# Choosing experts during cross-attention and scattering token records with indirect stores, in a decoder layer on one Trainium2 core

## The chip, the cores and the metric

The kernel runs on one core of a Trainium2 chip. The metric is the time of one execution on the device in microseconds (us), lower is better. A core has TensorE (PE; its weight loads are listed as PEld), VectorE (DVE), ScalarE (ACT) and GpSimd (POOL), each with its own instruction stream, and a queue SP (SyncE) that only issues DMAs. POOL also issues DMAs, among them the indirect ones, whose rows are picked by a list of indices in SBUF. Work on different engines is ordered by semaphores alone.

## What is computed

A decoder layer over 16 sequences ("rows") of 256 tokens with 256 features: local and global self-attention, then cross-attention to 120 context positions per row, then a mixture of experts. Only the last part and the way into it matter here. With x the tokens after cross-attention:

```python
xf = layernorm(x).reshape(-1, 256)             # 4096 tokens
logits = xf @ router_w.T                       # 8 experts
probs = softmax(logits)
top_p, top_i = top_k(probs, 2)
top_p = top_p / sum(top_p)                     # the two shares of a token
cw = sum(top_p[..., None] * one_hot(top_i, 8), axis=1)
for e in range(8):
    h = silu(xf @ w1[e].T) * (xf @ w3[e].T)
    out = out + cw[:, e:e + 1] * (h @ w2[e].T)
x = x + out
```

## The kernel before

Four stages follow one another, each a block at whose end all engines meet: `self_attention`, `cross_attention`, `route`, `expert_tiles`, and a last copy of the sums to the output.

`cross_attention` runs a software pipeline over rows b = 0 to 17; every engine has its own hand-written order of calls in that loop (`sync_program`, `gpsimd_program`, `tensor_program`, `scalar_program`, `vector_program`). In iteration b the scores of row b are made in four units s = 0 to 3: PE `scores` (L1201), DVE `maxima` (mask L1486, row maximum L1489), PE `subtract_max` (L1208), ACT `exponentials` (L1383), PE `turn` and `values` (L1221, L1233). Row b-1 is finished beside it: `divide`, `turn_att`, `project`, `residual` (DVE L1506). Row b-2 is normalised for the experts on POOL (`row_deviations` L1116, `apply_row_norm` L1127), turned (`turn_row` L1263), and multiplied by the router weights (`logits` L1276, in spare columns of a score bank). DVE's `copy_logits` (L1466) is put in front of `maxima(b, 0)` and takes row b-3. The query of row b+2 is split in three bf16 parts on POOL (L1140 to L1144), stored by SP (L1045), and loaded back in a stacked form (`stack_q`, L1038); `scores(b + 1, 0)` on PE comes right after `logits(b - 2)` and waits for the stacked loads of its row. SP also loads masks, expert weights and values, stores the rows for the experts, and in its iteration 4 issues eight small DMAs of `load_routing` (L1024 to L1032).

`route` (L1569) starts when all 4096 x 8 logits are in SBUF. DVE forms probabilities, takes the top two (L1661, L1664), makes one-hot rows `hot`, and with two PE products counts how many tokens of each expert come before each token; a prefix sum and the starts of the experts' regions give every token a slot in a list of 71 tiles of 128 slots (each expert's part is padded to whole tiles). Then token number and share are moved to their slots by one-hot products: for four groups of 16 token columns DVE builds `tile_hot` (L1712), `lane_hot` (L1714) and `entry` (L1717), POOL the second half of `entry` (L1621), and PE adds up 64 products (L1635). The results are `slot_row` (which token is in a slot, L1728), `slot_share`, and `tile_expert`. Nearly every DVE operation is wrapped in `step`, which makes the next one wait for its end.

`expert_tiles` handles the 71 tiles in order: POOL gathers 128 token rows (L1769), PE computes (L1807 to L1835), DVE scales by the share, and POOL adds the result to the sums with an indirect accumulating store (L1783). It can't start until `slot_row` is complete.

## Time and profile before

| | us |
|---|---|
| median of 3 runs | 1341.86 (1338.96 to 1342.02) |
| the profiled execution, its own time | 1334.86 |
| its span in the profile | 1332.9 |
| PE busy | 1164.3 (87%) |
| DVE busy | 604.5 (45%) |
| POOL busy | 593.7 (45%) |
| ACT busy | 523.9 (39%) |

The span is the time from the first to the last instruction of the profile; the stages stand in it one after the other, so a share of busy time over the whole span says little of any one of them. The profile's page cuts the span in 40 slices of 33.3 us each:

```profile
PE   3699999999999984899999994369999999999991
DVE  1355655556554541777777774832112211211220
POOL 6433444333443105466666422334555555555541
```

Each digit is the busy share of one slice in tenths. Cross-attention fills about slices 16 to 24, `route` most of slice 25 and part of 26, the experts the rest.

### The profile page before, as it was taken

To read this page: it belongs to the slowest core of one execution; us is meant where nothing else is said; L and a number is where in the kernel's file an instruction comes from. 1 tells how busy PE (TensorE), PEld (TensorE's weight loads), DVE (VectorE), ACT (ScalarE), POOL (GpSimd) and SP (SyncE) were. 2 spreads that over 40 slices of the span, in tenths; PEclk is the share of its full clock that TensorE was granted. 3 is DMA by queue.
4 is the path that set the end of the run, shared out by engine and by line. 5 is a ranking of instruction groups with operands and counts; after the bars stand their busy time and mean duration, and the time that the engine had idled before them with its cause. 6 is when DMAs were issued, how large, how long until landed. Compare 5 with 4: busy or idle time off the path is not lost. (4 is left out here: it accounts for less than half of the span.)

```text
span 1332.9 us, 27531 instructions
## 1 busy us (share of the span) xinstructions
PE 1164.3 (87%) x10384; PEld 873.8 (66%) x10384; DVE 604.5 (45%) x1081; ACT 523.9 (39%) x841; POOL 593.7 (45%) x800
## 2 busy tenths in 40 slices
PE   3699999999999984899999994369999999999991
PEld 2578787887888773677777773346666666666660
DVE  1355655556554541777777774832112211211220
ACT  1355555455554541666666651012222222222220
POOL 6433444333443105466666422334555555555541
PEclk9699999999999997899999997689999999999996
DMA  6472442625425105566666641002222222222224
GB/s 175 142 185 81 120 139 58 178 78 137 116 65 154 37 2 147 164 180 185 178 183 176 196 130 56 0 20 40 45 44 48 48 44 45 48 48 43 45 40 138
DMA packets 171325, 131.87 MB, mean 99 GB/s; under 512 B 58784, under 2 KB 160672, under 8 KB 171136
## 3 DMA queue, kind: packets, MB, share of 16 engines
q1 hardware_dynamic: 155216, 108.76, 29.4%
q0 software_dynamic: 13632, 18.62, 8.6%
q10 hardware_dynamic: 2352, 2.75, 0.7%
q8 instruction: 87, 1.43, 0.5%
q14 instruction: 38, 0.31, 0.1%
HBM read 90.31 MB, written 43.97 MB: 101 GB/s over the span
## 5 line engine op out<-in xcount | busy, mean ns | idle before, releaser
L704 ACT ACTIVATE sa_probs<-ps_scores 128x1024 f32<-128x1024 f32 x128 | 131.1, 1024 | 158.9 <-PE ps_scores L451 158.8
L1783 POOL DMA_INDIRECT sum_rows<-y,to_row x71 | 113.6, 1600 | 179.1 <-DVE y L1891 166.4
L1884 DVE TENSOR_TENSOR gate<-ps_scores,silu 128x512 f32<-128x512 f32 x71 | 49.1, 692 | 263.4 <-ACT silu L1862 263.4
L1862 ACT ACTIVATE silu<-ps_scores 128x512 f32<-128x512 f32 x71 | 42.4, 598 | 315.8 <-PE ps_scores L1817 315.8
L1817 PE MATMUL ps_scores<-w1s,xgT 128*128 x284 | 135.4, 600 | 2.3 <-ACT xgT L1856 2.3
L1835 PE MATMUL ps_out<-xres,ggT 128*128 x568 | 134.6, 380 | 1.6 <-DVE y L1891 1.6
L1817 PE MATMUL ps_scores<-w3s,xgT 128*128 x284 | 133.5, 592 | 0.0
L1835 PEld LDWEIGHTS ps_out<-xres,ggT 128*128 128x128 f32 x568 | 102.4, 190 | 13.2 <-issue 2.2
L837 DVE TENSOR_REDUCE sa_rowmax<-ps_scores 128x8 bf16<-128x1024 f32 x64 | 78.3, 1224 | 67.2 <-PE ps_scores L437 67.2
L837 DVE TENSOR_REDUCE sa_rowmax<-ps_turn 128x8 bf16<-128x1024 f32 x64 | 78.4, 1225 | 57.5 <-PE ps_turn L442 56.8
L1817 PEld LDWEIGHTS ps_scores<-w3s,xgT 128*128 128x128 f32 x284 | 54.1, 191 | 68.4 <-issue 68.4
L1486 DVE COPY_PREDICATED_SCALAR ps_scores<-zero,masked_score 128x960 f32 x64 | 77.2, 1207 | 17.2 <-PE ps_scores L1201 17.1
L451 PE MATMUL ps_scores<-neg_ident,sa_rowmax 128*128 128x128 bf16 x1024 | 79.6, 221 | 4.8 <-DVE sa_rowmax L837 4.8
L1383 ACT ACTIVATE xa_probs<-ps_scores 128x960 f32<-128x960 f32 x64 | 62.3, 973 | 54.6 <-PE ps_scores L1208 54.0
L1769 POOL DMA_INDIRECT xg<-xn_rows,from_row x71 | 71.9, 1013 | 22.1 <-POOL from_row L1765 20.0
L1817 PEld LDWEIGHTS ps_scores<-w1s,xgT 128*128 128x128 f32 x284 | 54.2, 192 | 41.2 <-issue 37.6
L285 POOL TENSOR_SCALAR rstd<-mv 128x2 f32<-128x2 f32 x16 | 3.6, 224 | 170.3 <-DVE mv L813 170.3
L1489 DVE TENSOR_REDUCE xa_rowmax<-ps_scores 128x8 bf16<-128x960 f32 x64 | 74.1, 1158 | 2.2
L1891 DVE TENSOR_SCALAR y<-ps_out,tile_share 128x256 f32<-128x256 f32 x71 | 34.3, 484 | 80.3 <-PE ps_out L1835 71.1
L1221 PEld LDWEIGHTS ps_turn<-ident,xa_probs 128*120 128x120 f32 x512 | 60.2, 138 | 11.1 <-issue 0.4
L451 PEld LDWEIGHTS ps_scores<-neg_ident,sa_rowmax 128*128 128x128 bf16 x1024 | 63.8, 99 | 5.3 <-DVE sa_rowmax L837 5.3
L1221 PE MATMUL ps_turn<-ident,xa_probs 128*120 128x128 f32 x512 | 67.1, 274 | 0.0
(210 smaller groups left out, 2368.9 us busy)
## 6 DMA issues: line engine op xcount, KB each, us to landing
xqs<-q_scr SPq DMA_DIRECT2D x96, 128.0 KB, 2.6
qs<-w_scr SPq DMA_DIRECT2D x42, 256.0 KB, 4.1
ks<-w_scr SPq DMA_DIRECT2D x42, 256.0 KB, 4.0
q_scr<-qp SPq DMA_DIRECT2D x16, 384.0 KB, 3.8
xks<-k_scr SPq DMA_DIRECT2D x48, 120.0 KB, 3.3
w_scr<-wp SPq DMA_DIRECT2D x7, 768.0 KB, 3.7
gs<-g_scr SPq DMA_DIRECT2D x48, 96.0 KB, 2.5
w1s<-in_w1T SPq DMA_DIRECT2D x16, 256.0 KB, 3.7
```

What stands on the lines that cost most here:

```text
L451: mm = pe.matmul(m.scores[s % 2][:, h, :], rowmax[s % 2][:, h:h + 1].broadcast_to((P, P)), m.neg_ident[:], start=False, stop=(h % 4 == 3), ...
L704: act.activation(probs[s % 2][:], m.scores[s % 2][:], ACT.Exp, scale=SCALE).then_inc(exped, 1)
L837: dve.tensor_reduce(rowmax[s % 2][:], m.turn[:] if kind else m.scores[s % 2][:], AX_X, ALU.max)\
L1221: mm = pe.transpose(m.turn[0:KX, h, :], probs[s % 2][:, h, 0:KX], m.ident[:])
L1383: act.activation(probs[s % 2][:, :, 0:KX], m.scores[s % 2][:, :, 0:KX], ACT.Exp, scale=SCALE)\
L1486: dve.copy_predicated(sc, zero[b % 2][:, n, :].unsqueeze(1).broadcast_to((P, HU, KX)), masked_score[:].unsqueeze(2).broadcast_to((P, HU, K ...
L1489: dve.tensor_reduce(rowmax[s % 2][:], sc, AX_X, ALU.max).then_inc(maxed, 1)
L1769: pool.indirect_dma_start(xg[i][:], None, m.xn_rows, bass.IndirectOffsetOnAxis(ap=from_row[i][:], axis=0))\
L1783: pool.indirect_dma_start(m.sum_rows, bass.IndirectOffsetOnAxis(ap=to_row[i][:], axis=0), y[i][:], None, compute_op=ALU.add).then_inc(y_ad ...
L1817: mm = pe.matmul(h_ps[r % 2][:, j:j + 1, :], xgT[r % 2][:, k, :], w[:, bass.ds(expert * DT + k, 1), :], start=(k == 0), stop=(k == DT - 1))
L1835: mm = pe.matmul(y_ps.unsqueeze(1), gT[r % 2][:, k, :], m.w2s[:, bass.ds(expert * HT + k, 1), :], start=(k == 0), stop=(k == HT - 1))
L1884: dve.tensor_tensor(gate[r % 2][:], h_ps[r % 2][:, 1, :], silu[r % 2][:], ALU.mult).then_inc(gate_done, 1)
```

## The change

Routing is spread over cross-attention. Tokens are taken in nine batches: (0,1), (2,3), ... (12,13) of two rows each, and rows 14 and 15 alone. For each batch k:

- DVE `choose(k)`: the top two logits of each token tile, their numbers, the difference of the two logits (the share is formed from it later), one-hot rows, their sum `sel`. It stands after `maxima(b, 3)` in the even iterations b = 4 to 14.
- PE `count(k)`: in bf16, one product with a triangular matrix and some with ones (8 for two rows, 4 for one), after `logits(b - 2)` and before `scores(b + 1, 0)` in the same iterations; it waits for `choose(k)`.
- DVE `copy_counts(k)` in front of `maxima` of the next row, and `place(k)` after `maxima(b, 2)` in the odd iterations: slots within fixed regions, 32 tiles for each expert.
- POOL `dispatch(k, i)`: for each row four indirect stores (two token tiles, two choices) of 128 records of 8 bytes (token number, logit difference) into a DRAM table, at the end of its iterations 5 to 16; 64 in all.

The last three batches are handled at the loop's end. The table is first filled with blank records (three stores of SP in iteration 2), `load_routing` moves from SP's iteration 4 to 0, and POOL gets `set_tables` in iteration 1. `route` keeps only: tiles of each expert from the running counts, the list of table tiles in use, one indirect gather of 71 table tiles, two PE transposes, and the shares from the logit differences.

```diff
         def load_routing():
...
+        def store_blank():
+            tab = m.table.rearrange("(r l) c -> r (l c)", l=P)
+            sp.wait_ge(blank_made, 1)
+            for r in range(0, N_TAB, P):
+                n = min(P, N_TAB - r)
+                sp.dma_start(tab[r:r + n, :], blank[0:n].rearrange("p l c -> p (l c)")).then_inc(spares_stored, 16)
@@ sync_program
-            if b == 4:
+            if b == 0:
                 load_routing()
+            if b == 2:
+                store_blank()
@@ gpsimd_program
+        def dispatch(k, i):
+            r0, rows = batches[k]
+            pool.wait_ge(slotted, k + 1)
...
+            for t in range(NT * (r0 + i), NT * (r0 + i + 1)):
+                for j in range(TOP):
+                    pool.indirect_dma_start(m.table, bass.IndirectOffsetOnAxis(ap=slot_i[:, t, j:j + 1], axis=0),
+                                            m.rec[:, t, j, :], None).then_inc(m.dispatched, 16)
@@
+            if b == 1:
+                set_tables()
+            if 5 <= b <= NB:
+                dispatch((b - 5) // 2, (b - 5) % 2)
+            if b == NB:
+                dispatch(LAST - 2, 0)
+                dispatch(LAST - 2, 1)
+        dispatch(LAST - 1, 0)
+        dispatch(LAST, 0)
@@ tensor_program
+        def count(k):
...
+            pe.wait_ge(chosen, k + 1)
+            pe.wait_ge(exped, min(UPR * (r0 + 4) + 3, UPR * NB))
+            pe.matmul(space(1, T), before[:], sel[:, 0:T, :], start=True, stop=False, skip_group_check=True)
+            for t in range(T - 1):
+                pe.matmul(space(2 + t, T - 1 - t), ones[:], sel[:, t:t + 1, :].broadcast_to((P, T - 1 - t, E)),
+                          start=False, stop=(t == T - 2), skip_group_check=True)
+            for t in range(T):
+                mm = pe.matmul(space(0, 1), ones[:], sel[:, t:t + 1, :], start=(t == 0), stop=(t == T - 1),
+                               skip_group_check=True)
+            mm.then_inc(counted, 1)
@@
+            if b == NB + 1:
+                count(LAST - 1)
...
                 values(b - 1, 3)
+            if b == NB:
+                count(LAST - 2)
             if done:
                 turn_row(b - 2)
...
                 logits(b - 2)
+            if 4 <= b < NB and b % 2 == 0:
+                count(b // 2 - 2)
             if more:
                 scores(b + 1, 0)
...
+        count(LAST)
@@ vector_program
+        def choose(k):
...
+            for t in range(T):
+                ins = dve.max(top[:, t, :], logit[:, t0 + t, :])
+            step(ins)
+            for t in range(T):
+                ins = dve.max_index(top_id[:, t, :], top[:, t, :], logit[:, t0 + t, :])
+            step(ins)
+
+            dve.tensor_tensor(m.rec[:, t0:t0 + T, 0, 1:2], top[:, 0:T, 0:1], top[:, 0:T, 1:2], ALU.subtract)
+            dve.tensor_tensor(m.rec[:, t0:t0 + T, 1, 1:2], top[:, 0:T, 1:2], top[:, 0:T, 0:1], ALU.subtract)
+            step(dve.tensor_copy(idf[:, 0:T, :], top_id[:, 0:T, 0:TOP]))
+            step(dve.tensor_tensor(hot[:, 0:T].rearrange("p t j e -> p (t j) e"),
...
+            dve.tensor_tensor(sel[:, 0:T, :], hot[:, 0:T, 0, :], hot[:, 0:T, 1, :], ALU.add).then_inc(chosen, 1)
+
+        def place(k):
...
+            step(dve.tensor_tensor(posn[:, 0:T, :], counts[:, 1:1 + T, :],
+                                   m.base[:].unsqueeze(1).broadcast_to((P, T, E)), ALU.add))
+            step(dve.tensor_tensor(m.base[:], m.base[:], counts[:, 0, :], ALU.add))
...
+            dve.tensor_copy(slot_i[:, t0:t0 + T, :], slotf[:, t0:t0 + T, :]).then_inc(slotted, 1)
@@
+            if b == NB:
+                choose(LAST - 2)
             if old:
                 divide(b - 1, 0)
...
                 maxima(b, 2)
+            if 5 <= b < NB and b % 2 == 1:
+                place((b - 5) // 2)
             if old:
                 residual(b - 1, 0)
             if some:
                 maxima(b, 3)
+            if 4 <= b < NB and b % 2 == 0:
+                choose(b // 2 - 2)
+            if b == NB:
+                copy_counts(LAST - 2)
+                place(LAST - 2)
             if old:
                 divide(b - 1, 1)
...
+        choose(LAST - 1)
+        copy_counts(LAST - 1)
+        place(LAST - 1)
+        copy_logits(NB - 1)
+        choose(LAST)
+        copy_counts(LAST)
+        place(LAST)
@@ route, gpsimd_program
+        pool.wait_ge(source_done, 1)
+        pool.wait_ge(m.dispatched, 16 * TOP * TILES)
+        pool.indirect_dma_start(records[:].rearrange("r l c -> r (l c)"), None, m.table.rearrange("(r l) c -> r (l c)", l=P),
+                                bass.IndirectOffsetOnAxis(ap=source_i[0:N_ST, :], axis=0)).then_inc(records_in, 16)
@@ route, tensor_program
+        pe.wait_ge(records_in, 16)
+        pe.transpose(ids_ps, records[:, :, 0], m.ident[0:N_ST, 0:N_ST])
+        pe.transpose(z_ps, records[:, :, 1], m.ident[0:N_ST, 0:N_ST]).then_inc(turned, 1)
```

## Rows read from the trace of the kernel before

**Rows 1.** Windows of the three stages: stretch, length, engines' busy us (count), clock, DMA.

```profile
525.00:823.00 298.00, 271.21 (x2856) 213.91 (x2856) 208.91 (x356) 180.82 (x251) 155.88 (x178) 0.97 0.58 167
823.00:880.00 57.00, 22.00 (x132) 20.28 (x132) 49.09 (x162) 0.42 (x1) 16.34 (x5) 0.66 0.00 1
880.00:1310.00 430.00, 416.49 (x1562) 259.65 (x1562) 83.46 (x142) 97.34 (x214) 221.29 (x355) 0.99 0.27 44
```

**Rows 2.** Timeline at the ends of route: start, us, engine, line, operation [idle <-releaser].

```profile
822.75 0.17 DVE L1466 COPY logits<-ps_scores 128x16 f32<-128x16 f32 x1 [7.39 <-PE ps_scores L1276]
...
841.23 0.17 DVE L1684 TENSOR_SCALAR count_i<-scan 128x8 int32<-128x8 f32 x1
841.43 0.17 DVE L1685 TENSOR_SCALAR tiles_i<-count_i 128x8 int32<-128x8 int32 x1
...
879.44 0.20 DVE L1728 TENSOR_SCALAR slot_row<-empty 128x71 int32<-128x71 f32 x1
880.15 0.19 POOL L1765 COPY from_row<-slot_row 128x1 int32<-128x1 int32 x1 [7.07 <-SPq L1899]
```

**Rows 3.** Groups of VectorE's instructions in route: line, shapes, count, busy us, mean ns.

```profile
L1664 DVE FIND_INDEX8 top_id<-top,prob 128x8 uint32<-128x8 f32 x32 | 4.4, 160 | 0.0
...
L1661 DVE MAX8 top<-prob 128x8 f32<-128x8 f32 x32 | 2.3, 152 | 0.0
```

**Rows 4.** Timeline of one steady row, PE and DVE around `scores(b + 1, 0)`.

```profile
695.09 0.42 DVE L1506 TENSOR_TENSOR xres<-ps_misc,xres 128x256 f32<-128x256 f32 x1 [2.54 <-PE ps_misc L1253]
...
696.67 1.16 DVE L1489 TENSOR_REDUCE xa_rowmax<-ps_scores 128x8 bf16<-128x960 f32 x1
...
697.33 0.96 PE L1276 MATMUL ps_scores<-routerT_sb,xbT 128*128 128x8 f32 x8
...
698.14 0.58 PE L1201 MATMUL ps_scores<-xks,xqs 96*128 96x120 bf16 x8
...
698.81 0.17 DVE L1466 COPY logits<-ps_scores 128x16 f32<-128x16 f32 x1 [0.36 <-PE ps_scores L1201]
...
701.90 0.43 DVE L1506 TENSOR_TENSOR xres<-ps_misc,xres 128x256 f32<-128x256 f32 x1 [0.59 <-PE ps_misc L1253]
```

**Rows 5.** Timeline, `copy_logits` of rows 5, 8 and 9: idle time before it.

```profile
664.78 0.17 DVE L1466 COPY logits<-ps_scores 128x16 f32<-128x16 f32 x1 [1.83 <-PE ps_scores L1201]
...
716.68 0.17 DVE L1466 COPY logits<-ps_scores 128x16 f32<-128x16 f32 x1 [1.22 <-PE ps_scores L1201]
...
734.09 0.17 DVE L1466 COPY logits<-ps_scores 128x16 f32<-128x16 f32 x1 [0.75 <-PE ps_scores L1201]
```

**Rows 6.** Timeline of one row, POOL's wait before a row, the split, SP's store.

```profile
703.48 0.23 POOL L1116 TENSOR_SCALAR brstd<-bmv 128x2 f32<-128x2 f32 x1 [5.23 <-DVE bmv L1476]
...
731.17 1.17 POOL L1144 TENSOR_TENSOR qp<-xrest,qp 128x512 bf16<-128x512 f32 x1
...
735.10 0.42 SPq L1045 DMA_DIRECT2D q_scr<-qp  x1
```

**Rows 7.** The two indirect DMAs by line: ns min/median/max; and landing.

```profile
L1769 POOL DMA_INDIRECT xg<-xn_rows,from_row x71: 974/1012/1242, 880.9 to 1284.6; - x71
...
DMA to landing us min/median/max: 2.7/2.8/3.5
...
L1783 POOL DMA_INDIRECT sum_rows<-y,to_row x71: 1562/1601/1644, 904.4 to 1308.9; - x71
...
DMA to landing us min/median/max: 3.5/3.8/4.0
```

**Rows 8.** Timeline of the last rows of cross-attention, VectorE and POOL.

```profile
804.48 0.25 DVE L1495 RECIPROCAL xrec<-ps_misc 128x16 f32<-128x16 f32 x1
...
805.73 2.44 POOL L1127 TENSOR_SCALAR xb<-xres,bmv,brstd 128x256 f32<-128x256 f32 x2
...
815.39 0.23 POOL L1116 TENSOR_SCALAR brstd<-bmv 128x2 f32<-128x2 f32 x1 [7.21 <-DVE bmv L1476]
...
816.52 2.44 POOL L1127 TENSOR_SCALAR xb<-xres,bmv,brstd 128x256 f32<-128x256 f32 x2
```

More of the change, by code:

```diff
@@ L962, in cross_attention @@
     zeros = sb("zeros", [P, D])
+    before_f = sb("before_f", [P, P])
+    before, ones = sb("before", [P, P], BF16), sb("ones", [P, P], BF16)
+    iota_p = sb("iota_p_sb", [P, P])
+    token1 = sb("token1_sb", [P, TILES])
+    blank = sb("blank", [P, P, 2])
+    logit = sb("logit", [P, TILES, E])
+    top = sb("top", [P, R * NT, E])
+    top_id = sb("top_id", [P, R * NT, E], U32)
+    idf = sb("idf", [P, R * NT, TOP])
+    hot, place_of = (sb(n, [P, R * NT, TOP, E]) for n in ("hot", "place_of"))
+    sel = sb("sel", [P, R * NT, E], BF16)
+    counts = sb("counts", [P, 1 + R * NT, E])
+    posn = sb("posn", [P, R * NT, E])
+    slotf = sb("slotf", [P, TILES, TOP])
+    slot_i = sb("slot_i", [P, TILES, TOP], I32)
     xb = [sb(f"xb{i}", [P, NT, D]) for i in range(2)]
@@ L1485, in maxima @@
                 copy_logits(b - 3)
+            if s == 0 and b > 4 and b % 2 == 1:
+                copy_counts((b - 5) // 2)
             dve.copy_predicated(sc, zero[b % 2][:, n, :].unsqueeze(1).broadcast_to((P, HU, KX)),
@@ L1581, in route @@
[L1581 to L1585 removed]
+    room = sb("room", [P, E])
     count_i = sb("count_i", [P, E], I32)
     tiles_i = sb("tiles_i", [P, E], I32)
[L1588 removed]
+    tiles_e = sb("tiles_e", [P, E])
@@ L1589, in route @@
     cum = [sb("cum0", [P, E]), sb("cum1", [P, E])]
+    behind = sb("behind", [P, E])
+    skipped = sb("skipped", [P, E])
+    lane = sb("lane", [P, 1])
+    source = sb("source", [P, 1])
+    source_i = sb("source_i", [P, 1], I32)
     passed = sb("passed", [1, N_ST, E])
     expert_f = sb("expert_f", [1, N_ST, 1])
-    lane_hot = [sb(f"lane_hot{i}", [P, GROUP, P]) for i in range(2)]
-    tile_hot = [sb(f"tile_hot{i}", [P, GROUP, N_ST]) for i in range(2)]
-    entry = [sb(f"entry{i}", [P, GROUP, 2, N_ST]) for i in range(2)]
@@ L1624, in tensor_program @@
[L1624 to L1637 removed]
+    records = sb("records", [N_ST, P, 2])
```

229 lines of the change are left out of this document (95 added, 134 removed).

## The prediction

> **What bounds the kernel now.** I first cut the span into stages with the view of windows [rows 1]. In cross-attention PE is busy for 271 of 298 us at nearly the full clock: it is the bound there. In the routing stage (823 to 880) VectorE is busy for 49 of 57 us and PE for 22, with DMA at 0.00: a stage bound by a chain of VectorE steps. In the experts' stage PE is busy for 416 of 430 us. So a change in `route` is worth what it takes from that stage's 57 us, and anything put into cross-attention costs in full where it makes PE wait.
>
> Next, the timeline at the ends of `route`. The last `copy_logits` starts at 822.75 and ends at 822.92; the last DVE step that makes `slot_row` is at 879.44, and the first instruction of the experts' stage, POOL's copy of the indices, starts at 880.15 [rows 2]. Between 822.92 and 880.15 lie 57.2 us. The end of that stretch is what the change moves; the experts' work behind it is not touched (same 71 tiles), so it moves as one block.
>
> **What `route` still costs.** Its DVE part up to the list of table tiles is a chain of 17 small steps (`room`, `lane`, `count_i`, `tiles_i`, `tiles_e`, a copy, six of the prefix sum, and five for `source_i`). Two such steps of the old chain start 0.20 us apart [rows 2]: 17 x 0.205 = 3.5 us, with some 0.3 us for the block's begin. Then the gather of 71 table tiles: an indirect gather costs POOL 1.0 us and lands 2.8 us after issue, 3.5 us at most [rows 7]; with the way to PE I take 3.2. Two small transposes: 0.7. Then nine short operations with one on ACT among them, `slot_row` to the last share: 2.3 us by the same step and a little more for 71 columns. From that to the experts' first copy 0.5, as now (879.64 to 880.15) [rows 2]. Together 10.5 us in place of 57.2, a gain of 46.7, if nothing were added elsewhere.
>
> **What is added behind row 15.** Here the chain gets longer, and the price of an indirect store to 8-byte records decides; the trace has none such. The nearest rows are the gather at 1.01 us and the accumulating store of 1 KB rows at 1.60 us [rows 7]. It can't be had for nothing, since POOL builds 128 descriptors in either; so 1.0 to 1.6, and I take 1.2: it has no accumulation and one small piece a record, which is nearer to the gather. Walked through with the times of before [rows 8]:
> - `choose(6)` now stands ahead of `divide(15, 0)` at 804.48, but row 14's norm is started at once and ends at 805.73 + 2.44 = 808.17. POOL then has `dispatch(5, 1)`, 4 stores, 4.8 us, to 813.0. `dispatch(6)` needs `place(6)`, which stands behind choose, count and `residual(15, 0)`, at about 812.4: ready in time. Its 8 stores take 9.6 us, to 822.6.
> - Only then come `row_deviations(15)` and `apply_row_norm(15)`, which before ran from 815.39 to 818.96, 3.57 us [rows 8]: now they end at 826.2, 7.2 us later. Before, the way from there to the last logits in SBUF was 822.92 - 818.96 = 4.0 us: 830.1.
> - `choose(8)` for two tiles 1.4 us, `count(8)` 0.7, `copy_counts` and `place(8)` 1.4: 833.6. `dispatch(8)`, 4 x 1.2 us: 838.5. `dispatch(7)` fits before it (826.2 to 831.0).
>
> So `route` starts at 838.5 in place of 822.9, and the experts at 838.5 + 10.5 = 849.0 in place of 880.15: 31.1 us earlier. The last store lands, by the longer row of 3.8 us, about 841.1; the wait for it is hidden behind the 17 steps, which end at 842.3. Sixteen stores are on this path (4 + 8 + 4), so 1.0 or 1.6 us a store gives -34.3 or -24.7.
>
> **What is added to the row loop.** One row takes 17.0 us. DVE has three waits for PE in it, 2.54, 0.59 and 0.36 us, 3.5 in all [rows 4].
> - `place(k)` (five steps, 1.1 us) falls into the wait of 2.54, `copy_counts` into that of 0.59: nothing, and if the first cover were gone, 1.1 us each for six batches.
> - `choose(k)` with `count(k)` is another matter. DVE ends the row maximum of unit 3 at 696.67 + 1.16 = 697.8. `choose` then has 4 maxima and 4 index searches: 2.3 us for 32 is 0.07 each after a first of 0.15, and 4.4 for 32 is 0.14 each [rows 3]: 0.38 + 0.65, then two subtractions, a copy, the one-hot rows and `sel`, 0.2 each with the step's gap: 1.9 us, to 699.6, and 0.1 to PE. But PE has the logits of row b-2 from 697.33 on and starts `scores(b + 1, 0)` at 698.1 [rows 4]. Queued behind the wait on PE are these scores and all after them, for which ACT and DVE wait in turn. So PE stands 1.6 us and spends about 0.7 on eight bf16 products of at most 32 columns (the row at 698.14 is eight larger ones, 0.58 us). 2.4 us in each of six batches: +14.4. Bounds: 1.9 if `choose` is shorter, 4 if the delayed `divide` and maxima pass the delay on.
> - Something comes back. `scores(b + 1, 0)` now sometimes waits for the stacked queries: `copy_logits` has 1.83, 1.22 and 0.75 us of idle before it where the usual value is 0.36, 2.7 us too much in all [rows 5, 4]. `load_routing` leaves SP's iteration 4, ahead of these places, and PE's rows get longer while SP's work does not, so these waits go: -2.7 (bounds 0 and -2.7). In iterations 0 and 2 SP gets eleven issues more, of 0.42 us or so each [rows 6], some 5 us; SP waits for POOL's split there and no `copy_logits` has come yet. I cost them at nothing; without that cover a late query would cost up to 5 us once.
> - `dispatch` in the loop: 4 stores a row, 4.8 us, against POOL's wait of 5.23 us before the next row's norm [rows 6]: nothing. If a store costs more, there are 2.8 us further before SP waits for the split (732.34 to 735.10 [rows 6]): it bites from (5.2 + 2.8) / 4 = 2.0 us a store.
> - `set_tables` (five short operations) and two memsets lie in POOL's waits too: nothing.
>
> **Sum**, on the profiled execution of 1334.86 us: -31.1 + 14.4 - 2.7 = -19.4, that is 1315.5. The median of the runs shown is 7.0 us above it; on it the change gives 1341.9 - 19.4 = 1322.5.
>
> **Rivals.**
> 1. *The stores starve.* POOL's descriptors for an indirect store advance only while VectorE is idle. In the trace indirect DMAs run only in the experts' stage, where VectorE is busy for 83 of 430 us [rows 1]; in cross-attention it is busy for 209 of 298. Idle there are 3.5 us a row [rows 4], less 1.6 for half a batch of choosing and placing: 1.9, while four stores need at least 4.1. Each of twelve rows would stretch by 2.2 us, at 2.6 us a store: +26, 1349. It turns the change into a loss from 2.4 us a store on in the loop, (2.4 - 2.0) x 4 x 12 = 19. Against it: VectorE's long operations in the row loop, mask and row maximum, work on PSUM, and so did the one beside which the stores of the experts' stage held their 1.6 us. The Trainium skill has this as a rule (SBUF — State Buffer, section "SBUF: two separate sides": while VectorE runs an operation in a mode with two ports, GpSimd is locked out and can't write descriptors; the section after it has such a DMA go from about 0.62 to 3.1 us). By that figure, an estimate of that page, four stores would take 12.4 us a row and the kernel would be slower; no row of this case shows the lock, since no indirect DMA here runs beside such an operation.
> 2. *The delay spreads.* DVE has 3.5 us of slack in a row, of which `choose` takes 1.9 at one place, ahead of `divide(b - 1, 1)`; if PE then waits again for `att` or the maxima, a batch costs 4 us in place of 2.4: +9.6, 1332. For it: the two engines hand work to and fro in every unit. Against it: PE's own delay of 2.4 us covers the 1.9 of DVE.
> 3. *The count is nearly free.* If PE makes up the standing time by working off what it was late with (its 271 of 298 us leave 27 [rows 1]), six batches cost 0 to 1 us each: 1310. Against it: most of those 27 us are in the last rows, where nothing is left to make up with.
> 4. *It doesn't do what it says*: the experts start hardly earlier, because the gather from the table or a late store takes the place of the one-hot products; it would need over 20 us there: 1342.
>
> **How the numbers follow.** Forecast 0.60, rival 1 0.11, rival 2 0.13, rival 3 0.10, rival 4 0.06. The forecast's own bounds: 1.0 us a store and 1.9 us a batch, 1322.5 - 3.2 - 3.0 = 1316; 1.6 a store and nothing back from SP, 1322.5 + 6.4 + 2.7 = 1332. The range reaches into rivals 2 and 3 and, with the scatter of the runs shown (3 us), becomes 1308 to 1337; left out are rivals 1 and 4 and the edge of the others, 0.19. A measurement of this kernel can tell about 0.3%, 4 us, from no change. Faster: forecast, rivals 2 and 3, a little of 4: 0.83. Same: 0.07. Slower: 0.10.
>
> **What would show it.** In the profile of the changed kernel: the experts' first gather 12 to 25 us earlier; between the last logits and it some 20 us; PE idle of 1 to 2 us ahead of `count` six times, with "chosen" by DVE as the releaser; POOL's indirect stores at 1.0 to 1.6 us each, back to back behind row 14's norm; no wait of POOL over budget, that is the norm of the next row starting without delay. I am wrong if a store takes over 2 us, if a pair of rows grows by 4 us or more, or if `dispatched` is waited for at length in `route`.

## The result, and the profile after it

The changed kernel takes 1360.2 us (median, 1354.1 to 1365.9), the kernel before 1340.6 beside it: ratio 1.0146, 95% interval 1.0095 to 1.0197. It is slower by some 20 us where 19 less were forecast. The profiled execution took 1362.9 us, its span is 1361.0.

The view of windows by stage, as [rows 1]: stretch, length, busy us of PE, its weight loads, DVE, ACT, POOL, then clock, DMA share, GB/s.

```profile
531.00:879.20 348.20, 293.94 (x2916) 229.42 (x2916) 232.72 (x534) 182.19 (x251) 215.88 (x242) 0.89 0.54 144
879.20:910.00 30.80, 0.77 (x6) 0.51 (x6) 9.51 (x45) 0.26 (x1) 6.88 (x6) 0.50 0.03 5
910.00:1340.00 430.00, 416.33 (x1562) 259.63 (x1562) 83.43 (x142) 97.40 (x214) 220.98 (x355) 0.99 0.27 44
```

The routing stage fell from 57 to 31 us. Cross-attention grew from 298 to 348: PE has 23 us more of busy time at a mean clock of 0.89 instead of 0.97, and 27 us more of standing. The experts' stage has the same length.

The timeline of the changed kernel around a choice and its count (start, us, engine, line, operation, idle time before it and its releaser), which answers to [rows 4]:

```profile
616.20 1.16 DVE L1636 TENSOR_REDUCE xa_rowmax<-ps_scores 128x8 bf16<-128x960 f32 x1
...
616.85 0.96 PE L1342 MATMUL ps_scores<-routerT_sb,xbT 128*128 128x8 f32 x8
617.27 0.36 DVE L1583 MAX8 top<-logit 128x8 f32<-128x8 f32 x4
...
618.96 0.19 DVE L1598 TENSOR_TENSOR sel<-hot 128x32 bf16<-128x32 f32 x1
...
619.25 0.18 PE L1357 MATMUL ps_scores<-sel,before 128*128 128x32 bf16 x1 [1.45 <-issue]
...
619.61 0.58 PE L1265 MATMUL ps_scores<-xks,xqs 96*128 96x120 bf16 x8
...
620.66 1.66 PE L1285 MATMUL ps_turn<-ident,xa_probs 128*120 128x128 f32 x8
...
624.94 0.42 DVE L1653 TENSOR_TENSOR xres<-ps_misc,xres 128x256 f32<-128x256 f32 x1 [2.06 <-PE ps_misc L1317]
```

The choice takes DVE from 617.27 to 619.15, the 1.9 us that were costed. PE stands 1.45 us and counts in 0.4. Behind that its granted clock falls: it is 1.00 up to 620.60 and 0.59 from there to 622.40, in part the lower of its two levels (1.2 instead of 2.4 GHz). Eight transposes take 1.66 us there, which take 1.03 in a row without a count.

From one `residual` to the next a row has two segments, 10.2 and 6.8 us long in the kernel before (the short one in [rows 4], 695.09 to 701.90). Some of them in the changed kernel, by windows (columns as above):

```profile
674.45:687.30 12.85, 8.75 (x82) 6.75 (x81) 5.85 (x8) 5.84 (x8) 7.73 (x8) 0.87 0.66 183
687.30:697.50 10.20, 10.02 (x103) 7.74 (x101) 7.45 (x15) 6.81 (x10) 7.49 (x9) 1.00 0.39 111
697.50:707.88 10.38, 8.91 (x90) 7.12 (x89) 7.56 (x27) 4.34 (x6) 7.02 (x8) 0.84 0.81 164
...
718.07:731.09 13.02, 9.58 (x82) 7.38 (x81) 5.86 (x9) 5.41 (x8) 7.73 (x8) 0.74 0.76 210
...
761.82:770.90 9.08, 7.19 (x86) 5.84 (x84) 5.76 (x8) 4.30 (x6) 7.01 (x8) 1.00 0.85 258
770.90:782.49 11.59, 10.86 (x95) 8.69 (x96) 7.56 (x15) 7.44 (x11) 7.50 (x9) 0.85 0.41 113
```

Three patterns stand here. 697.50 is the short segment of a row with a count, 10.4 us instead of 6.8. At 674.45 and 718.07 there is no count, and the segment has 12.9 and 13.0 us. From 761.82 on a pair has 9.1 and 11.6 in place of 6.8 and 10.2. Set beside the segments of the kernel before, the loop from the first `residual` of the second row to the last one is 45.0 us longer: 20.7 in the six segments with a count; 10.8 in the two long ones; 7.9 in two pairs of the third kind; 5.7 in the rest.

What lies behind the long segments is on SP. Its timeline ahead of the first of them (the issues of the DMA queue) and PE's first late scores, and then SP's waits (total us, times, longest), the last line that of the kernel before:

```profile
637.80 0.40 SPq L1076 DMA_DIRECT2D q_scr<-qp  x1
649.74 4.68 SPq L1069 DMA_DIRECT2D xqs<-q_scr  x5
...
658.61 11.68 SPq L1069 DMA_DIRECT2D xks<-k_scr  x6
...
671.61 0.38 SPq L1076 DMA_DIRECT2D q_scr<-qp  x1
675.09 4.65 SPq L1069 DMA_DIRECT2D xqs<-q_scr  x6
...
681.93 0.61 PE L1265 MATMUL ps_scores<-xks,xqs 96*128 96x120 bf16 x8 [2.52 <-DMA xqs<-q_scr]
```

```profile
SPq L1069 <- DMA q_scr<-qp: 76.9, 15, 11.5
SPq L1069 <- DMA xks<-k_scr: 22.9, 10, 4.1
...
SPq L1038 <- DMA q_scr<-qp: 61.2, 16, 7.4
```

SP sends the split queries to the scratch tensor and waits for the confirmation before it reads them back stacked. At 637.80 it waits 11.5 us (in the kernel before 7.4 at most). All that it does is then late: the keys until 670.3, the next row's queries only at 671.61, and PE waits for them at 681.93. The same happens from 683.52 (stacked from 692.50 on) to the scores at 724.90. The copies of logits behind these scores stood idle for 3.27 and 4.18 us, where [rows 5] show 0.75 to 1.83.

The windows of that wait (columns as above, the last two DMA share and GB/s), the last line being of the kernel before, behind its store at 652.74:

```profile
641.00:644.00 3.00, 2.06 (x18) 1.58 (x18) 1.53 (x4) 0.92 (x2) 1.94 (x3) 1.00 0.70 207
...
645.00:649.70 4.70, 4.54 (x47) 3.45 (x46) 4.60 (x9) 3.80 (x6) 4.01 (x6) 1.00 0.00 0
...
656.10:656.70 0.60, 0.60 (x5) 0.49 (x3) 0.60 (x1) 0.27 (x1) 0.60 (x1) 1.00 0.10 28
```

For the last 4.7 us of the wait the profile shows no packet under way; only the confirmation is missing. In the kernel before SP goes on at 656.68, when the transfers have only just ended.

The tail, from POOL's timeline and then all engines, which answers to [rows 8] and [rows 2]:

```profile
856.44 1.09 POOL L1180 DMA_INDIRECT table<-rec,slot_i  x1 [0.18 <-issue]
...
870.49 0.96 POOL L1180 DMA_INDIRECT table<-rec,slot_i  x1 [0.30 <-issue]
...
879.03 0.17 DVE L1559 COPY logit<-ps_scores 128x16 f32<-128x16 f32 x1 [9.99 <-PE ps_scores L1342]
...
882.13 0.17 DVE L1611 CAST slot_i<-slotf 128x4 int32<-128x4 f32 x1
...
886.37 0.96 POOL L1180 DMA_INDIRECT table<-rec,slot_i  x1 [0.30 <-issue]
895.25 0.17 DVE L1781 TENSOR_SCALAR room<-iota_e_sb 128x8 f32<-128x8 f32 x1 [12.96 <-PEq L1703]
...
898.52 0.16 DVE L1797 TENSOR_TENSOR source_i<-source,lane 128x1 int32<-128x1 f32 x1
...
898.99 2.08 POOL L1760 DMA_INDIRECT records<-table,source_i  x1 [11.66 <-DVE source_i L1797]
...
906.44 0.40 PE L1765 MATMUL ps_misc<-ident,records 71*128 71x71 f32 x1 [25.42 <-DMA records<-table,source_i]
...
910.05 0.19 POOL L1848 COPY from_row<-slot_row 128x1 int32<-128x1 int32 x1 [8.98 <-SPq L1982]
```

Twelve stores stand back to back ahead of row 15's norm, 1.27 us apart. The last store ends at 887.33, and the routing stage's first step starts at 895.25. The gather is issued at 898.99 and PE has its records at 906.44.

### The profile page after: what moved, and what is told of

Its sections match the earlier page's. It is cut to its first block and busy times, and to the rows that moved or that the text cites. A ratio compares the mean times of both kernels' runs of the same rounds, so it can differ in the third digit from the quotient of the medians.

```text
span 1361.0 us, 27550 instructions
## 1 busy us (share of the span) xinstructions
PE 1171.1 (86%) x10318; PEld 872.8 (64%) x10318; DVE 588.7 (43%) x1141; ACT 525.3 (39%) x841; POOL 644.1 (47%) x867
## 5 line engine op out<-in xcount | busy, mean ns | idle before, releaser
L1633 DVE COPY_PREDICATED_SCALAR ps_scores<-zero,masked_score 128x960 f32 x64 | 77.3, 1207 | 18.5 <-PE ps_scores L1265 18.4
L1285 PEld LDWEIGHTS ps_turn<-ident,xa_probs 128*120 128x120 f32 x512 | 67.1, 150 | 17.6 <-issue 9.1
L1285 PE MATMUL ps_turn<-ident,xa_probs 128*120 128x128 f32 x512 | 75.0, 295 | 3.1 <-ACT xbT L1502 3.1
L1180 POOL DMA_INDIRECT table<-rec,slot_i x64 | 63.6, 994 | 22.6 <-issue 16.9
L1484 ACT COPY xa_probsT<-ps_turn 120x1024 f32<-120x1024 f32 x64 | 64.8, 1012 | 13.6 <-PE ps_turn L1285 12.8
```

The lines of the kernel that those rows point to most:

```text
L1180: pool.indirect_dma_start(m.table, bass.IndirectOffsetOnAxis(ap=slot_i[:, t, j:j + 1], axis=0), m.rec[:, t, j, :], None).then_inc(m.dispat ...
L1285: mm = pe.transpose(m.turn[0:KX, h, :], probs[s % 2][:, h, 0:KX], m.ident[:])
L1484: act.copy(probsT[s % 2][0:KX, :, :], m.turn[0:KX, :, :]).then_inc(turn_read, 1)
L1633: dve.copy_predicated(sc, zero[b % 2][:, n, :].unsqueeze(1).broadcast_to((P, HU, KX)), masked_score[:].unsqueeze(2).broadcast_to((P, HU, K ...
```

## The experiments

Each kernel was timed beside the kernel before; ratios are to that one, with the 95% interval. Kernels with less work or other data in the table say so in their expectation.

### Which part of the change costs: stores or choice

**The stores of the loop left out** (`e1_no_loop_stores`):

```
-            if 5 <= b <= NB:
-                dispatch((b - 5) // 2, (b - 5) % 2)
```

> The changed kernel without the 48 indirect stores of batches 0 to 5 (the records of rows 0 to 11 are missing from the table, so most tokens get no expert); choose, count and place stay as they are, and the last 16 stores too. Theory A (the 8-byte stores are confirmed late, and SP's store of the query parts, issued beside them, is confirmed late with them, so the next row's scores wait): in the trace of the changed kernel the odd iterations take up to 6 us more than before; they return to 17.0 us, SP waits about 4 us for each store of the query parts in place of 9 to 12, and the time falls by about 20 us, from 1360 to 1340. Rival B (SP is late because choosing and counting shift the row loop, with or without stores): within 5 us of 1360. The even iterations keep their 3.6 us more under both.

Measured: 1332.7 us, 0.996 (0.993 to 0.999). The segments are 10.2 to 10.4 with a count and 6.8 without (8.0 once); SP's waits for `q_scr` are 56.6 us, longest 6.2. So the 48 stores cost some 27 us although POOL has the time for them. By the traces 24 of these are in the loop: 12.2 in the two segments in which SP's confirmation is late, 8.3 in the pairs of the third kind, the rest in small pieces.

**The choice, count and placing of the loop left out** (`e2_no_loop_choose`), the stores kept and sent to places fixed beforehand:

```
-            if 4 <= b < NB and b % 2 == 0:
-                choose(b // 2 - 2)
```

> The changed kernel with all 64 stores, but without choose, count, copy_counts and place for rows 0 to 11, whose records go to fixed slots spread over the eight regions (so the routing of these rows is not computed). Theory A: the even iterations lose their 3.6 us more (six times, 21.6 us), the odd ones keep waits for stacked queries; SP still waits 9 to 12 us for the store of the query parts; time about 1340. With PE's rows shorter these waits could even grow. Rival B: with choosing and counting gone, SP is in time again, and the time is about 1318.

Measured: 1377.2 us, 1.0305 (1.027 to 1.034), slower than with the choice, and pairs of segments of 20 to 24 us instead of 17. That went against any theory in which a store has one price. What the stores cost depends on where their records go.

**The choice one place earlier** (`e3_choose_early`): behind `maxima(b, 2)` and `place`, ahead of `residual(b - 1, 0)`:

```
+            if 4 <= b < NB and b % 2 == 0:
+                choose(b // 2 - 2)
             if old:
                 residual(b - 1, 0)
             if some:
                 maxima(b, 3)
-            if 4 <= b < NB and b % 2 == 0:
-                choose(b // 2 - 2)
```

> The changed kernel, complete, with choose(k) moved ahead of residual(b - 1, 0), into VectorE's wait of 2.5 us, so that count(k) finds it done. If the order wait is the cause of the even iterations' 3.6 us (1.6 of standing, 0.7 of products, the rest PE at the half clock after it): they fall to 0.5 to 1 us, -16 us, 1344. If SP's late stacked queries are a bound of their own, part of it returns as longer waits there: 1350. If the order wait is not the cause: 1360.

Measured: 1350.5 us, 1.0095 (1.007 to 1.012). The segments with a count fall to 7.0 to 8.1 us (one to 10.1), but others rise to 13.8, and SP's waits for `q_scr` to 93.9 us. DVE can hide the choice; a part of what that frees goes into SP's lateness.

### Where the records lie

**Records 64 bytes apart** (`e5_pitch64`) instead of 8; the gather at the end still takes whole rows of the table, now 71 of 8 KB:

```
+PITCH = 16
-        m.table = nc.dram_tensor("table", [N_TAB * P, 2], F32, kind="Internal").ap()
+        m.table = nc.dram_tensor("table", [N_TAB * P, PITCH], F32, kind="Internal").ap()
-            dve.tensor_copy(slot_i[:, t0:t0 + T, :], slotf[:, t0:t0 + T, :]).then_inc(slotted, 1)
+            dve.tensor_scalar(slot_i[:, t0:t0 + T, :], slotf[:, t0:t0 + T, :], float(PITCH // 2), None, ALU.mult)\
+                .then_inc(slotted, 1)
```

> The changed kernel, complete, with the table's records 64 bytes apart in place of 8 (still 8 bytes written in each; the blank fill and the last gather move eight times the bytes, some 3 us more at the end). If the late confirmation comes from neighbouring records that share a line of memory: SP's wait for the store of the query parts returns to 4 us, the end of cross-attention passes soon after the last store in place of 8 us later, and the time falls by 20 us to 1340. If it comes from the smallness or the number of the writes: as the changed kernel, 1360 to 1365.

Measured: 1358.8 us, 1.0162 (1.011 to 1.021), no gain in sum. But the segments without a count are 6.8 to 7.1 us again once the stores run, SP's waits 57.6 us, the last logits at 859.96. The gain went into the gather (trace of `e5_pitch64`, the line's time to landing):

```profile
DMA to landing us min/median/max: 26.3/26.3/26.3
```

**The same with fixed places** (`e6_fixed_pitch64`), meant to tell a shared 64-byte line from the pattern of the places:

> The kernel of e2_no_loop_choose (stores to fixed places, the choice, count and placing of batches 0 to 5 left out, so the table is not the reference's), with records 64 bytes apart as in e5_pitch64. Theory: what holds SP's scratch stores back is 8-byte records of one 64-byte line written by one indirect store from several DMA engines. Then the rows of the loop, 20 to 24 us in e2, fall back to about 17, the copy of the last logits comes near 835 to 845 instead of 891.8, and the gather of 71 rows of 8 KB takes back about 20: 1325 to 1345. Rival: the fixed places are slow for another reason (two records of a token 512 places apart, the regions' offsets): the rows stay over 20 us, and with the long gather the time is 1385 to 1400.

Measured: 1397.5 us, 1.0453 (1.041 to 1.049). The edit did not do what its expectation says: the fixed places were not multiplied by the new distance, so the records of the loop still lay 8 bytes apart, as in `e2_no_loop_choose`, and only the gather grew by its 20 us, the difference of the two kernels. Before I saw that, it set me on the theory that the regions' distance of 32 KB was the cause, and three kernels went to it.

**Regions 37 KB apart** (`h1_stride37`, `CAP = TOKENS // P + 5`); the same in `e6_fixed_pitch64`; and `e2`'s fixed places with the choice kept:

> The changed kernel with one number changed: the regions of the table start 37 KB apart (CAP = 37 rows of 1 KB) instead of 32 KB, records still 8 bytes apart; the fill of the table is 330 rows instead of 295. e6 showed that stores to fixed places are slow at 64 bytes too, so sharing a line is not the whole cause. Theory L (records of one line): the regions' distance does nothing, 1355 to 1365, SP's waits for the scratch store 75 us or more. Theory S (the eight regions lie a power of two apart, so the records of one store fall on the same part of the memory): the loop is as in e1 and e5, SP's waits near 57 us, last logits near 860 us, and with the short gather 1338 to 1345.

> e6_fixed_pitch64 (fixed places, 64 bytes apart, choice, count and placing of batches 0 to 5 left out, the table is not the reference's) with the regions 37 rows of 8 KB apart instead of 32. Theory S: the fixed places of e6 lie exactly a power of two apart, and this ends it: 1397 falls to 1330 to 1350. If the fixed places are not the cause, but the choice that was left out, the time stays at 1385 to 1400. Theory L says nothing on this pair and would be left with two causes.

> The changed kernel whose stores of batches 0 to 5 go to e2's fixed places (8 bytes apart, regions 32 KB apart), while choice, count and placing are kept and their places go to a tile that nobody reads (the table is not the reference's). If the places are what made e2_no_loop_choose (1377) slower than the changed kernel (1360): 1375 or more, since the choice's own cost comes on top. If leaving out the choice did it (rows that run at another pace meet the stores otherwise): 1355 to 1365.

Measured: 1350.6 us, 1.0075 (1.005 to 1.010); 1397.3, 1.0418 (1.036 to 1.048); 1385.7, 1.0336 (1.028 to 1.040). The third shows that the places, not the missing choice, made `e2_no_loop_choose` slow. The second has the time of `e6_fixed_pitch64`, but that does not show that the distance does nothing: the segments of 14 to 16.5 us of `e6_fixed_pitch64` are down to a single one of 18.2, and in their place stand eight pairs of about 9.1 and 11.5 us, the third pattern above, of which `e6_fixed_pitch64` has none. The first is 10 us below the changed kernel and between both expectations, with five such pairs; what the distance does stays open.

**Fixed places truly 64 bytes apart, and side by side.** `i1_fixed_apart64` multiplies them; in `i2_fixed_linear8` the 128 records of a store lie in one piece of 1 KB:

> e2_no_loop_choose (stores of batches 0 to 5 to fixed places, their choice, count and placing left out, the table is not the reference's) with all records 64 bytes apart, the fixed places too: in e6_fixed_pitch64 these had stayed 8 bytes apart. Theory L (records of one store that share 64 bytes hold up the other stores' confirmation): all rows of the loop take about 17 us, SP's waits for the scratch store are near 57 us, the last logits come near 835 us, and with the gather of 71 long rows, some 20 us, the time is 1330 to 1345. Rival P (the pattern of the fixed places is slow at any distance): 1385 to 1400.

> e2_no_loop_choose with other fixed places: the 128 records of a store lie side by side, 1 KB in one piece, 8 bytes apart (choice, count and placing of batches 0 to 5 left out as there). In e2 and here eight records share 64 bytes, but in e2 they come from partitions eight apart (p, p+8, ...), here from eight neighbouring ones. Theory L without regard to who writes: as e2, 1370 to 1385. If only records written by different DMA engines hurt, and neighbouring partitions are written by one engine: as without sharing, 1310 to 1325. If the eight regions, not the shared bytes, are the cause: 1310 to 1325 too, and i1 tells these apart.

Measured: 1358.9 us, 1.0155 (1.011 to 1.020), with the long gather (869.15 to 895.54); without its excess of 22 us it would be at 1337. And 1411.5 us, 1.053 (1.047 to 1.059). SP's waits, first of `i1_fixed_apart64`, then of `i2_fixed_linear8`:

```profile
SPq L1072 <- DMA q_scr<-qp: 63.8, 16, 6.3
```

```profile
SPq L1071 <- DMA q_scr<-qp: 100.9, 16, 16.1
SPq L1071 <- DMA xks<-k_scr: 52.3, 12, 11.8
```

The same choice of regions, the same number of stores and bytes, and 1397 falls to 1359. By this edit the regions lie eight times as far apart too, 256 KB, so it does not part the distance of the records from that of the regions. One region with eight records to 64 bytes is worse than eight such regions, so the regions are not needed for the harm, and that neighbouring partitions write them does not help.

### The kernels put together

**Choice early, a gather of 80 rows, and records 64, 32 and 16 bytes apart** (`f1_early_pitch64`, `f2_early_pitch32`, `f4_early_pitch16`); the new edit is the gather:

```
+N_GET = 80
-                                bass.IndirectOffsetOnAxis(ap=source_i[0:N_ST, :], axis=0)).then_inc(records_in, 16)
+                                bass.IndirectOffsetOnAxis(ap=source_i[0:N_GET, :], axis=0)).then_inc(records_in, 16)
```

> The changed kernel with three edits: choice of a batch one place earlier on VectorE (e3_choose_early), records 64 bytes apart (e5_pitch64), and the last gather over 80 rows of the table instead of 71, so that its rows can be shared out over the 16 DMA engines. Theory: the loop's loss is the sum of two causes, the count that waits for the choice (about 3.6 us in each of six rows, gone as in e3) and the shared lines (gone as in e5), and the 26.3 us landing of e5's gather is 71 rows on one DMA engine: it falls to 3 to 6 us. Then 1358.8 - 20 (gather) - 14 to 20 (choice) = 1316 to 1325, faster than the kernel before by 1 to 1.8%. Rival A: the gather's time is the table's bytes from DRAM, not the engine: landing stays over 15 us, 1335 to 1345. Rival B: what e3 gained in even rows comes back in odd ones whatever the pitch: 1332 to 1340.

> f1_early_pitch64 with records 32 bytes apart instead of 64. If a store only suffers from records that share 32 bytes or less, the loop is as in f1 and the gather and the fill of the table are half as long: 1314 to 1323. If two records to a 64-byte line are enough to hurt, SP's waits for the scratch store's confirmation come back, and the time is 1325 to 1345, with single odd segments over 8 us.

> f2_early_pitch32 with records 16 bytes apart instead of 32: four places to 64 bytes, of which one store fills about two, since first and second choices of a token go in different stores. Theory L, with a loss that grows with the number of records of one store in 64 bytes: between e3_choose_early (1350.5, four of eight places) and f2 (1319.5, about one): 1325 to 1340. If any distance over 8 bytes is enough: 1315 to 1320, the fastest kernel of the study.

| bytes | kernel | median us | ratio (interval) | SP's waits for `q_scr`, us |
|---|---|---|---|---|
| 8 | `e3_choose_early` (71 rows) | 1350.5 | 1.0095 (1.007 to 1.012) | 93.9 |
| 16 | `f4_early_pitch16` | 1326.7 | 0.9918 (0.990 to 0.994) | 77.2 |
| 32 | `f2_early_pitch32` | 1319.5 | 0.9878 (0.985 to 0.991) | 64.4 |
| 64 | `f1_early_pitch64` | 1325.7 | 0.9897 (0.986 to 0.994) | 71.6 |

From 8 to 16 bytes the time falls by 24 us and the waits by 17. Beyond that the steps are not told apart: `f4_early_pitch16` was measured on another occasion than the other two, and 32 bytes have waits of 64.4 here and 73.3 in `f3_early_pitch32_tail` (56.6 without the loop's stores). `f2_early_pitch32` is the fastest kernel of the study, 1.2% under the kernel before. 64 bytes bring nothing over 32; the table has twice the bytes and its gather takes 6.0 us instead of 4.1. In every one of these kernels the regions move apart with the records. The loop of `f2_early_pitch32` by windows:

```profile
681.83:688.84 7.01, 7.01 (x90) 5.83 (x89) 5.88 (x10) 4.63 (x6) 6.04 (x7) 1.00 0.73 195
688.84:699.04 10.20, 10.02 (x103) 7.74 (x101) 8.70 (x21) 6.81 (x10) 8.45 (x10) 1.00 0.63 183
699.04:705.85 6.81, 6.81 (x82) 5.62 (x81) 5.76 (x8) 4.63 (x6) 5.88 (x7) 1.00 0.97 292
```

The segment with a count takes 7.01 us, 0.2 more than one without, at the full clock.

**Four stores moved behind row 15's norm** (`f3_early_pitch32_tail`) and **37 KB with the choice early** (`h4_early_stride37`):

> f2_early_pitch32 with the stores of row 13 issued behind the norm of row 15 on GpSimd instead of ahead of it. In the changed kernel twelve stores (15.0 us) stand ahead of that norm, and four of them (5.1 us) are moved behind it. If that norm's start sets the last logits: 3 to 5 us less than f2. If the norm's other input or the stores behind it take over (the last store must land before the gather): 0 to 2 us less.

> The changed kernel with the choice one place earlier (e3), regions 37 KB apart, records 8 bytes apart, gather of 80 rows. Theory S: as f2_early_pitch32 or a little better, for gather and fill are a quarter of its: 1314 to 1322. Theory L: near e3_choose_early less the shorter gather, 1342 to 1350.

Measured: 1321.6 us, 0.9898 (0.987 to 0.993): nothing against `f2_early_pitch32`. And 1349.5 us, 1.0059 (1.003 to 1.009), as theory L has it. SP's waits for `q_scr` are 91.0 us, near the 93.9 of `e3_choose_early`, so its confirmation is still late. But this trace has eight of the unexplained stalls (below), which `e3_choose_early` and `f2_early_pitch32` don't have, so the time does not tell what the distance alone is worth.

**The gather alone** (`g1_gather80`), and **32 bytes with the choice in its place** (`g2_pitch32_gather80`), this one measured a second time, beside other runs of the kernel before (`g3_pitch32_gather80_again`):

> The changed kernel with one edit: the last gather reads 80 rows of the table instead of 71 (the table has 9 more rows, which nobody uses). If the 7.4 us landing of 71 rows is one DMA engine moving them all, 80 rows land in about 2.8 us as in h4_early_stride37: 4.5 us less than the changed kernel, 1354 to 1358. If the landing there was short for another reason: no change, 1358 to 1362.

> f2_early_pitch32 with the choice back in its place ahead of divide(b-1, 1), so the changed kernel with 32 bytes to a record and a gather of 80 rows. The loop then holds the cost of choice and count alone. e1_no_loop_stores has it too (even segments 10.2 to 10.4 instead of 6.8): 3.5 us in each of six rows, 21 us. So 1319.5 + 21 = 1336 to 1342. If choice and count cost what was predicted, 2.4 us in each row: 1332 to 1335. If something else, as the clock, takes part of it: below 1330.

> The kernel of g2_pitch32_gather80 once more, in another job. If the stalls that the trace calls remote belong to the job and not to the kernel: none in this trace, odd segments at 6.8 us, even ones at 10.2 to 10.4, and 1334 to 1340 (e5_pitch64's 1358.8 less 22 for its long gather is 1337). If they belong to the kernel: again five or more of them, and 1346 to 1356. A third outcome, stalls and all but in a job in which the kernel before is as slow as in g2's (1341), would leave it open.

Measured: 1357.4 us, 1.0122 (1.008 to 1.017), 2.8 us under the changed kernel, which the scatter doesn't separate; the landing itself is plain, 2.8 us (trace of `g1_gather80`):

```profile
DMA to landing us min/median/max: 2.8/2.8/2.8
```

Then 1350.7 us, 1.0068 (1.004 to 1.010), and for the same kernel the second time 1333.3 us, 0.9933 (0.991 to 0.996), while the kernel before had 1340.9 both times. The two traces, windows of `g2_pitch32_gather80` and of the second measurement, and VectorE's wait in the first:

```profile
704.95:715.14 10.19, 10.01 (x103) 7.73 (x101) 8.70 (x20) 7.11 (x11) 7.49 (x9) 1.00 0.64 192
715.14:724.20 9.06, 7.20 (x86) 5.83 (x84) 5.76 (x9) 4.73 (x6) 7.00 (x8) 1.00 0.31 89
724.20:735.86 11.66, 11.13 (x96) 8.93 (x97) 7.68 (x16) 6.90 (x10) 7.49 (x9) 0.85 0.74 185
...
DVE xres L1656 <- remote: 15.3, 5, 3.8
```

```profile
697.56:707.76 10.20, 10.03 (x104) 7.74 (x101) 8.70 (x21) 6.81 (x10) 7.50 (x9) 1.00 0.47 132
707.76:714.57 6.81, 6.81 (x82) 5.62 (x81) 5.76 (x9) 4.63 (x6) 5.88 (x7) 1.00 0.88 255
714.57:724.77 10.20, 10.02 (x103) 7.74 (x101) 7.45 (x15) 6.81 (x10) 8.60 (x11) 1.00 0.55 153
...
724.77:735.08 10.31, 8.86 (x90) 7.04 (x89) 7.64 (x26) 4.83 (x6) 6.99 (x8) 0.83 0.73 202
```

Behind a projection ("remote") PE and DVE stand for 2 to 3 us, which the trace gives to no engine, and the segment after it runs at a clock of 0.85. These pairs are in the changed kernel's trace too, from 761.82 on. VectorE's waits of this kind are two there, two in `g1_gather80`, five in `g2_pitch32_gather80`, and 5, 8, 2 and 8 in `h1_stride37` to `h4_early_stride37`; no trace of the e, f and i kernels has one. The same kernel has them on one occasion and not on another, and they cost it 17 us. It is not the chip alone that decides: the e kernels, without them, and the h kernels, with them, ran on a chip of the same number. All 32 of these waits stand in segments in which POOL issues its four stores; but `g3_pitch32_gather80_again` has stores from the same point of its segments on and no stall. So in these traces a stall needs the stores, and something of the occasion besides. The median of the kernel before, with no stores in its loop, shows no sign of them (no trace of it was taken beside these kernels). What they are stays open. It follows that kernels measured on different occasions can be compared to 15 us or so only: the 27 us above between the changed kernel and `e1_no_loop_stores` holds some of it. Measured on one occasion are `e1_no_loop_stores` to `e5_pitch64`, `e6_fixed_pitch64` with `f1_early_pitch64` to `f3_early_pitch32_tail`, and `i1_fixed_apart64` with `i2_fixed_linear8` and `f4_early_pitch16`, all without stalls; `h1_stride37` to `h4_early_stride37`, and `g1_gather80` with `g2_pitch32_gather80`, have them in different number, so that these compare less well even among themselves.

## Why the prediction was wrong

On the profiled execution the sum gave 1315.5 us, and it took 1362.9: 47.4 too little (37.7 on the medians; the profiled execution of before lay 7.0 under its median, that of after 2.7 over).

| step | predicted | measured | missed |
|---|---|---|---|
| up to the second row (self-attention not touched) | 0 | +5.6 | 5.6 |
| row loop | +11.7 | +45.0 | 33.3 |
| last `residual` to last logits | +7.2 | +5.7 | -1.5 |
| last logits to the experts' first copy | 18.9 | 30.9 | 12.0 |
| experts' stage | 0 | -1.8 | -1.8 |

- **Self-attention.** POOL's first instruction of cross-attention came at 512.95 instead of 507.16. Variants of the changed kernel, in which this stage is the same, have either value (`e1_no_loop_stores` 512.54, `e2_no_loop_choose` 505.62), so it is scatter between executions.
- **The step that failed is `dispatch` in the loop, put at nothing.** Its price was right: 1.27 us a store from start to start against 1.2, all 64 of them, and POOL still waits before the next row's norm, 0.8 us behind the first four stores and 2.4 to 5.5 behind the others of the loop. The reasoning asked only who waits for POOL. It did not ask what the records do to DMAs of others under way. SP's wait for the confirmation of the query store lies on the way to `scores(b + 1, 0)`, with few us to spare: [rows 5] showed it late three times already. I had read these as a reserve that would come back (-2.7); they were the sign that this path had no slack. In the changed kernel it is 10.8 us in two places by the trace. How much it is in all depends on the occasion. On those without the unexplained stalls 8 bytes cost 31.0 us against 32 with the choice early (`e3_choose_early` less `f2_early_pitch32`, some 3 of it the gather), and 38.6 against 64 with fixed places (`e6_fixed_pitch64` less `i1_fixed_apart64`, the same long gather); each of these pairs spans two occasions. The one pair that differs in nothing but the distance and was measured on one occasion, with stalls, gives only 6.7 (`g1_gather80` less `g2_pitch32_gather80`).
- **Why the confirmation is late** is shown only in part. Shown: it needs the stores, and it is worst with records 8 bytes apart, packed in one piece worst of all; at 16 bytes and more most of it is gone. The share of the regions' distance is not parted from this. Also shown: during the wait the DMA engines move nothing for the last 4.7 us (645.00 to 649.70), so that stretch is not one in which the queries are still being transferred, as far as the packets in the profile tell. The Trainium skill (DMA: Bandwidth & Descriptors, section "Queues, rings and completion order") states that the write that raises a DMA's semaphore lands only after every earlier write of the same DMA engine, across its queues. By that, SP's confirmation waits behind the slow small writes of POOL's queue, which agrees with 11.5 us of waiting for a store that elsewhere takes 4 to 7, and with the silent stretch at its end. That it is the small writes that are completed late, and not the queries' own, is argued and not shown.
- **Choice and count: +14.4 predicted, 20.7 measured** in the changed kernel and 20.0 in the undisturbed trace of `g3_pitch32_gather80_again`. Standing (1.6 predicted, 1.45 measured) and the count (0.7, 0.4) were right. The term left out is the clock: in the segment with a count it is 0.83 instead of 1.00, that is in part at 1.2 instead of 2.4 GHz, right behind the standing, and PE is busy 8.9 us for the work of 7.0. So it is 3.4 us a batch instead of 2.4. In medians it is 13.9 us between `g3_pitch32_gather80_again` (1333.3) and `f2_early_pitch32` (1319.5), on two occasions.
- **Rival 2** came nearest in size for a batch (4 us) and had the wrong reason. Rival 3 is refuted as it stood, but with the choice one place earlier count and choice are indeed nearly free, 0.2 us.
- **Rival 1**, the stores that starve beside VectorE, did not come: a store takes 0.96 us with VectorE busy for two thirds of the time (233 of 348 us). The rule that the prediction cites from the Trainium skill does not show in this kernel's row loop. The kernel is slower as that rival said, by another mechanism. **Rival 4** came in part: `route` takes 12.0 us more than forecast, where the rival asked for over 20.
- **The tail** went as walked through: twelve stores ahead of row 15's norm, four behind the last placing. That their number sets the end was wrong: with four of them moved away nothing was gained (1321.6 against 1319.5).
- **`route`: 18.9 predicted, 30.9 measured.** The 17 steps took 3.4 us (3.5). The gather took 7.4 us to PE instead of 3.2: I priced it by gathers of 128 rows, and this one has 71. With 80 rows, more bytes, it took 2.8. The Trainium skill (DMA: Bandwidth & Descriptors, section "Why a DMA increments its semaphore by 16 and not by 1") says that a DMA is shared out over the largest number of engines up to 16 that divides its rows: 1 for 71, 16 for 80; the two landings agree. The other 7.6 us lie ahead of `room`: that the wait for the last store's landing "is hidden behind the 17 steps" was wrong. Between the end of the last store on POOL and the first step stand 7.9 us here and 5.6 in `f2_early_pitch32` (842.51 to 848.11), where the kernel before, with no store under way, starts its first step (`tile`, L1653) at 823.24, 0.3 behind the last logits. It is 5.6 in thirteen of the nineteen kernels. Longer, 7.4 to 10.2, it is only in the six whose records all lie 8 bytes apart, in regions of 32 KB or in one piece, with the stores in the loop. With the regions 37 KB apart (`h1_stride37`, `h4_early_stride37`) it is 5.6 at 8 bytes too, so here their distance does count. I take this for the end of the block, which holds all engines until POOL's DMAs have landed; that was not tried by itself.

So the gain in `route` was real (57.2 to 30.9 us) and would have been larger with 80 rows; it went, and more with it, into the loop: the choice and its clock, a DMA confirmation on the critical path that the stores make late, and stalls whose cause is open. With 32 bytes to a record, 80 rows and the choice early, the idea of the change brings 1.2%.

## What to carry to other kernels

A small indirect store costs more than the time of the engine that issues it: ask which confirmation in flight is on the critical path, and do not pack the records of one store 8 bytes apart (32 were the fastest here; 16, 32 and 64 are not told apart). Give an indirect DMA a number of rows that 16 divides, even if the last rows are thrown away: 80 rows landed in 2.8 us, 71 in 7.4. Put work on which PE waits one place earlier than it is needed: PE standing for 1.5 us cost as much again in clock.

## What the runs showed of the hardware

- 128 records of 8 bytes in one piece of 1 KB were the worst: loop segments of up to 18.4 us and waits of 16.1 us for an unrelated 384 KB store (`i2_fixed_linear8`).
- A gather of 71 rows of 1 KB landed in 7.4 us and of 8 KB in 26.3; of 80 rows of 1 KB in 2.8, of 4 KB in 4.1, of 8 KB in 6.0.
- An indirect store of 128 8-byte records occupies POOL for 0.96 us, 1.27 from start to start, and from the end of the last one to the next block's first step stand 5.6 to 10.2 us.
- While SP waited for a late confirmation, the DMA engines stood at a share of 0.00 for 4.7 us (changed kernel, 645.00 to 649.70).
- The same kernel had 1350.7 and 1333.3 us on two occasions (intervals 1.004 to 1.010 and 0.991 to 0.996), while the kernel without these stores had 1340.9 on both.
